# GpSimd makes both halves' low parts for some experts of the first expert pass

## The reference

```python
def ffn(x, Wg, bg, W1, b1, W2, b2):          # 4096 tokens of 128, 8 experts, hidden 256
    xf = x.reshape(-1, 128)
    probs = softmax(xf @ Wg + bg)
    w, idx = top_k(probs, 2); w = w / sum(w)
    comb = sum(one_hot(idx, 8) * w[..., None], axis=1)
    h = relu(einsum('nd,edh->enh', xf, W1) + b1[:, None, :])
    y = einsum('enh,ehd->end', h, W2) + b2[:, None, :]
    return einsum('end,ne->nd', y, comb)

x = x + long_convolution(layernorm(x))       # FFT over 256 positions, 16 sequences
x = x + ffn(layernorm(x))                    # first expert pass
x = x + attention(layernorm(x))              # 16 heads of 8, 4 query sets, causal
x = x + ffn(layernorm(x))                    # second expert pass
```

## Time and profile before

| | us |
|---|---|
| median of 3 runs | 857.32 (856.18 to 859.0) |
| the profiled execution, its own time | 855.01 |
| its span | 853.3 |
| TensorE busy | 801.8 (94%) |
| VectorE busy | 682.4 (80%) |
| ScalarE busy | 719.8 (84%) |
| GpSimd busy | 550.3 (64%) |

### The profile page before, as it was taken

The page is one execution under the profiler, slowest core; times in us unless marked ns, Lnnn a source line. Parts: engine busy times, 40 slices in busy tenths (PEclk is TensorE's granted clock), DMA queues, the critical chain, the costliest instruction groups (busy, mean ns, idle before and its releaser), DMA issues.

```text
span 853.3 us, 20661 instructions
## 1 busy us (share of the span) xinstructions
PE 801.8 (94%) x7793; PEld 446.1 (52%) x7793; DVE 682.4 (80%) x2000; ACT 719.8 (84%) x919; POOL 550.3 (64%) x620
## 2 busy tenths in 40 slices
PE   5899898989999999999999999999999999999995
PEld 4644475666677623333333333333333677777774
DVE  6898699999998766777777777778736899888884
ACT  7640488778888899999999999999998889999984
POOL 1187455535553498988899888888887555454542
PEclk9999999999999999999999999999999999999998
DMA  8201100000003334343334433433420000000000
GB/s 263 69 1 49 50 2 1 2 2 2 2 1 77 95 70 98 87 86 89 100 101 100 100 96 90 97 87 91 98 41 2 1 14 15 14 14 14 14 14 17
DMA packets 38521, 46.20 MB, mean 54 GB/s; under 512 B 6696, under 2 KB 24368, under 8 KB 38416
## 3 DMA queue, kind: packets, MB, share of 16 engines
q1 hardware_dynamic: 38416, 44.83, 20.8%
HBM read 28.03 MB, written 16.78 MB: 53 GB/s over the span
## 4 chain that ended last, share of the span: by engine, by line
PE 61%; ACT 14%; DVE 13%; issue 9%; POOL 3%; SPq 0%; DMA 0%; ACTq 0%
PE psum L816 16%; PE psum L762 15%; PE psum L1114 12%; ACT prob L1072 11%; PE psum L1063 5%; PE psum L1172 4%; DVE mixed L828 3%; DVE normed L351 2%; PE psum L566 2%; POOL prob L1087 2%; ACT decay L420 1%; PE psum L956 1%; PE psum L533 1%; PE psum L637 1%; DVE hidden_parts_first L785 1%
## 5 line engine op out<-in xcount | busy, mean ns | idle before, releaser
L1072 ACT ACTIVATE prob<-psum 128x1536 f32<-128x1536 f32 x256 | 347.7, 1500 | 15.5 <-PE psum L1063 15.5
L1114 PE MATMUL psum<-prob,vstack 128*32 128x256 f32 (+1 forms) x2048 | 204.9, 495 | 1.6 <-DVE o_tok L1122 1.6
L762 PE MATMUL psum<-xt_parts,w_parts 128*128 128x512 f16 x768 | 186.6, 379 | 0.0
L828 DVE SCALAR_TENSOR_TENSOR mixed<-psum,comb_y,mixed 128x128 f32<-128x128 f32 x512 | 143.1, 339 | 2.1 <-PE psum L816 2.1
L792 POOL TENSOR_TENSOR hidden_parts_second<-hidden_second,hidden_parts_second 128x512 f16<-128x512 f32 x64 | 78.9, 1233 | 91.8 <-ACT hidden_parts_second L778 91.8
L792 POOL TENSOR_TENSOR hidden_parts_first<-hidden_first,hidden_parts_first 128x512 f16<-128x512 f32 x64 | 77.9, 1222 | 77.7 <-ACT hidden_parts_first L778 77.5
L776 ACT ACTIVATE hidden_first<-psum,b 128x512 f32<-128x512 f32 x128 | 88.3, 690 | 29.1 <-PE psum L762 22.0
L1082 POOL TENSOR_SCALAR_AFFINE_SELECT prob<-prob 128x512 f32<-128x512 f32 x128 | 82.4, 644 | 41.0 <-ACT prob L1072 35.5
L1063 PE MATMUL psum<-qstack,kstack 32*128 32x512 f16 x768 | 99.7, 385 | 9.7 <-POOL prob L1087 4.8
L1063 PEld LDWEIGHTS psum<-qstack,kstack 32*128 32x128 f16 x768 | 24.9, 91 | 158.2 <-ACT prob L1072 139.8
L816 PE MATMUL psum<-w_parts,hidden_parts_first 128*128 128x128 f16 x1536 | 96.0, 219 | 10.5 <-DVE mixed L828 5.7
(11 more groups left out here) (121 smaller groups left out, 1101.1 us busy)
## 6 DMA issues: line engine op xcount, KB each, us to landing
qstack<-qk_parts SPq DMA_DIRECT2D x128, 128.0 KB, 3.6
qk_parts<-parts SPq DMA_DIRECT2D x64, 192.0 KB, 3.2
kstack<-qk_parts SPq DMA_DIRECT2D x128, 32.0 KB, 3.5
stream<-L_attn_a_u SPq DMA_DIRECT2D x4, 512.0 KB, 8.4
kept_x<-stream SPq DMA_DIRECT2D x4, 512.0 KB, 2.6
out<-mixed SPq DMA_DIRECT2D x8, 256.0 KB, 2.3
w_whole<-L_ffn_W SPq DMA_DIRECT2D x1, 1024.0 KB, 7.6
taps<-c_taps SPq DMA_DIRECT2D x1, 640.0 KB, 9.8
```

The source lines that it names most:

```text
L762: last = e.matmul(bank(u % 4), m.w1[:, w_part, ex, cols], xt_parts[:, s, x_part, :], start=(n == 0), stop=(n == len(PRODUCTS) - 1))
L828: last = e.scalar_tensor_tensor(out=m.y[:, t0 + t, :], in0=bank(down_bank(m, i))[:, t * P:(t + 1) * P], scalar=comb_y[:, s, t, ex:ex + 1], ...
L1072: e.activation(prob[:, n % PROBS, :], psum[:, TILE * (n % 2):TILE * (n % 2 + 1)], ACT.Exp, scale=SCALE)\
L1114: last = e.matmul(to[SLOT * lane:SLOT * (lane + 1)], vstack[:, b % 2, keys, first:first + SLOT], weights_of(n - t, lane, keys, pair), star ...
```

## The change

For some experts of the first pass GpSimd makes the low parts of both halves with one instruction of 128x1024 elements, which counts `low_both_halves`, and VectorE's instruction is left out. These are experts 3 and 6 in chunks 0 to 5, and experts 1, 3, 5 and 7 in chunks 6 and 7, 20 of 64. GpSimd's instruction keeps its place in the queue and its wait for the second half's relu. TensorE waits for the one semaphore instead of the two; where it waits for the two, it counts only the experts that use them. The second pass is as before.

```diff
--- before.py
+++ after.py
@@ -287,6 +287,7 @@
     combt_up, combt_copied, base_up, based = (sem(n) for n in ("comb_t_up", "comb_t_copied", "base_up", "based"))
     hid_up, relued, low_first, low_second, down_up, accum = (sem(n) for n in (
         "hidden_up", "relued", "low_first_half", "low_second_half", "down_up", "accumulated"))
+    low_both = sem("low_both_halves")
     STEPS = 14
     STACK = 2 * 2 * LANES * 16
 
@@ -778,8 +779,20 @@
                 last = e.activation(m.hidden_parts[:, r, 0, k, :], bank(u % 4), ACT.Relu, scale=scale, bias=bias)
             last.then_inc(relued, 1)
 
+
+    def both_on_gpsimd(i):
+        ch, ex = divmod(i, EXPERTS)
+        return ch < FFN_CHUNKS and (ex in (3, 6) if ch < FFN_CHUNKS - 2 else ex % 2 == 1)
+
+    def lows_before(i):
+
+        alone = sum(both_on_gpsimd(n) for n in range(i + 1))
+        return i + 1 - alone, alone
+
     def vector_low(e, m, ch, ex):
         i = (m.at + ch) * EXPERTS + ex
+        if both_on_gpsimd(i):
+            return
         r = i % HRING
         e.wait_ge(relued, HBLK * i + 1)
         e.tensor_tensor(m.hidden_parts[:, r, 1, 0, :], m.hidden[:, r, 0, :], m.hidden_parts[:, r, 0, 0, :],
@@ -789,8 +802,12 @@
         i = (m.at + ch) * EXPERTS + ex
         r = i % HRING
         e.wait_ge(relued, HBLK * i + 2)
-        e.tensor_tensor(m.hidden_parts[:, r, 1, 1, :], m.hidden[:, r, 1, :], m.hidden_parts[:, r, 0, 1, :],
-                        ALU.subtract).then_inc(low_second, 1)
+        if both_on_gpsimd(i):
+            e.tensor_tensor(m.hidden_parts[:, r, 1], m.hidden[:, r], m.hidden_parts[:, r, 0], ALU.subtract)\
+             .then_inc(low_both, 1)
+        else:
+            e.tensor_tensor(m.hidden_parts[:, r, 1, 1, :], m.hidden[:, r, 1, :], m.hidden_parts[:, r, 0, 1, :],
+                            ALU.subtract).then_inc(low_second, 1)
 
     def down_bank(m, i):
 
@@ -803,8 +820,12 @@
             e.wait_ge(relued, HBLK * (i + 1))
             terms = [(m.hidden[:, r, k], m.w2[:, ex * HBLK + k, :]) for k in range(HBLK)]
         else:
-            e.wait_ge(low_first, i + 1)
-            e.wait_ge(low_second, i + 1)
+            shared, alone = lows_before(i)
+            if both_on_gpsimd(i):
+                e.wait_ge(low_both, alone)
+            else:
+                e.wait_ge(low_first, shared)
+                e.wait_ge(low_second, shared)
             terms = [(m.hidden_parts[:, r, h_part, k], m.w2[:, w_part, ex * HBLK + k, :])
                      for k in range(HBLK) for h_part, w_part in PRODUCTS]
         if i >= 2:
```

## The result

The kernel after takes 864.5 us (median of 6 runs, 862.8 to 867.7), the kernel before 857.0 beside it (6 runs): ratio 1.0089, 95% interval 1.0067 to 1.0112. It is 7.5 us slower; the forecast was 867.6, 10.3 slower.

The account below looks back on a forecast made before the run. TensorE was taken to set the pace, with VectorE nearly full and partly waiting for GpSimd. Terms 5.1 + 3.2 + 0 + 1.0 + 1.0 = 10.3 us on a median of 857.3 gave 867.6 us, range 857 to 872.

Parts of the forecast that it names:

- What bounds the pass, and the lock: First expert pass: TensorE sets the pace, VectorE is nearly full and partly stands still until GpSimd's instruction ends.
- The exception kept from the earlier trace: GpSimd's rstd (L345) ran 1.05 us while two-input VectorE work (L683) passed; kept as ground for a rival.
- The joined instruction: GpSimd's 1024-element subtraction takes 2.13 us, 0.97 more than the 1.16 of a single half.
- the cheaper rival: Joined instruction at 1.7 us, so places cost about 0.5 each: 3.5 us slower, 861; chance 0.16.
- Expert 3, the first place: Chunks 1 to 5: L666 held 0.97 longer, routing chain 1.2 us late, L712 on TensorE 0.5 late.
- Expert 6, chunks 3 to 5: GpSimd's joined part delays VectorE's four L351 and what follows: 1.7 us a chunk, 5.1 for three.
- The new hole at down(7): Chunk 3: TensorE's down product of expert 7 waits for late L828 of expert 5, starting at 201.25, not 199.56.
- Chunks 1 and 2: Delays 1.24, 0.97 and 0.95 less 1.56 won from the blocked L785: 1.6 us late each, 3.2 together.
- Chunk 0, 6 and the end: Chunk 0 costs 0, at most 0.2; chunk 6 costs 1.0; the last down product in chunk 7 is 1.0 late.
- "faster": Rival: GpSimd lets VectorE in between the joined instruction's halves; 3.2 us won, 854.1; chance 0.13.
- "A wash": Rival: VectorE's saved 13.6 us and the added locks cancel everywhere but the last place: 858.3; chance 0.09.
- the hole at down(5): Chunks 3 to 5: TensorE waits 1.07 us for GpSimd's low part, queued behind L343 waiting for VectorE's statistics.

Follow-up runs that it names:

- extralow2: Kernel before plus a second full-size GpSimd subtraction (128x512) ahead of expert 3's low part in chunks 0 to 5, VectorE keeping its half: 857.63 us (1.0022).
- split: Kernel after with each joined GpSimd instruction written as two of 512 elements, one behind the other: 861.39 us (1.0052 to the kernel before).
- extrapow: Kernel before plus a GpSimd power on 128x4 elements behind expert 3's low part in chunks 0 to 5: 858.58 us (1.0012).
- lasttwo: Kernel after with only chunks 6 and 7 joined (experts 1, 3, 5 and 7), other chunks as before: 860.83 us (1.0038 to the kernel before).
- no7: Kernel after with the last expert of chunk 7 as in the kernel before: 864.28 us (1.0097 to the kernel before).

## Why the prediction was right, and where not

- *What bounds the pass, and the lock*: right. L667 ended 0.03 us behind GpSimd's joined instruction, at 1.64 us as said. By the rule of the Trainium skill that was weighed (page SBUF — State Buffer, section "SBUF: two separate sides"), the hold lasts for the whole instruction; extralow2 and split agree, with ends within 0.04 us. The exception kept from the earlier trace rows holds too: in extrapow a power with two SBUF inputs held none of five two-input instructions, so for it the measurement decides against the rule.
- *The joined instruction*: 2.13 forecast, 2.145 measured. The slope of the earlier trace rows was the right source; the cheaper rival, at 1.70, is out. The estimate from the Trainium skill's page GPSIMD Engine Reference, section "Elementwise — side-by-side cycle accounting", 2.29, was too high.
- *Expert 3, the first place*: the mechanism was right to each instruction, but L698 was 1.0 late, not 1.2. The forecast let the chain go on at 188.1, with 0.96 left, and wrote 189.3 for the sum, which is 189.06; the 1.24 that it took on to chunks 1 and 2 follows from neither. Measured from the mark, the chain ended at 12.14 us, 11.13 before. L712 then is 0.35 late, not 0.5. At down(5) this place has cost 0.71, where the forecast had 0.9.
- *Expert 6, chunks 3 to 5*: 1.7 forecast, 1.34, 1.18 and 1.35 measured. The mis-sized term is the length of the four L351: they begin 0.62 late (forecast 0.57), but take 3.78, not 4.15. GpSimd's row ended 0.32 sooner than forecast: 0.17 from the chain, the rest since one low part starts before the row of the one ahead ends (196.93, 198.04: 1.11 apart at 1.15 long). Over three chunks 3.9 in place of 5.1. The new hole at down(7) came; that at down(5) did not grow beyond the lateness that reaches it.
- *Chunks 1 and 2*: 1.6 forecast, 1.30 and 1.14 measured. At L828 of expert 4 it is 1.29 in chunk 2: 1.01 for the first place (forecast 1.24), and 0.28 for all of 0.97 + 0.95 - 1.56 (forecast 0.36).
- *Chunk 0, 6 and the end*: 0, and 1.86 for the last two against 2.0; TensorE waits 0.93 longer at L713 of chunk 6 and 1.07 at the last down, and all of it stays. Right, and lasttwo and no7 show them apart.
- *Sum*: 8.2 in the pass against 10.3, and every term that isn't zero a little too large. The profiled executions differ by 9.15 us, the medians by 7.5. The clock blurs the medians (last section): at a mean granted clock of 0.997 executions of the kernel before took 854.8 to 855.6 us and those of the kernel after 862.8 and 863.3, some 8 us more, as the marks say. Of the 3.1 us by which the forecast lies above the median, 2.1 is the sum and 1.0 this scatter.
- *The rivals*: "faster" needed L666 to end within 0.7 us; it took 1.64. Made to let go in the middle (split), the change loses 4.6 us still (3.6 by the marks), so that rival's price was wrong too. It had the first place at nothing, chunks 3 to 5 at -0.35 and the end at 1.0. In split the second half catches one more instruction of the chain (L673, 0.79 us) and the next low part an earlier one than before (L691, 1.03), so that the chain ends 0.50 late; L352 takes 3.66 in chunk 3, not 3.01, so down(7) waits for VectorE; and chunks 6 and 7 cost 1.8. "A wash" is out.

What the prediction did not see: the hole at down(5) that it described, with the row of three low parts behind it, was worth 9.2 us, more than the change costs, and one number removes both.

## What to carry to other kernels

Where two engines share a lock, work moved from one to the other is paid by both: price it by what the receiver's instruction will catch, not by the giver's busy time, part of which is waiting for that lock. If it must be moved, keep the seams, so that the other engine's short instructions get in. And look first for an instruction that stands too early in a queue, waits there, and keeps ready work behind it from starting: here moving two small steps by one expert gave 9.2 us, while the moved work cost 7.5.

## What the runs showed of the hardware that was not expected

A GpSimd subtraction on tiles of 128x512 stops VectorE's casts (L667, 128x8), its instructions with two inputs in SBUF (L673, 128x4) and the one-input scalings (L352, 128x128) until it ends. It does not stop the accumulation L849, one of whose two tiles is in PSUM: the four from 202.84 took 1.11 us beside a low part from 202.88 to 204.03. A GpSimd power of 128x4, over 1 us long, stops no two-input instruction (extrapow).

TensorE's granted clock dips right behind the pass in seven of the fourteen profiled executions, and this blurs the medians. In extrapow's profiled execution (window; PE, PEld, VectorE, ScalarE, GpSimd busy; granted clock; DMA share; GB/s):

```profile
296.34:301.34 5.00, 2.71 (x19) 1.03 (x18) 2.92 (x14) 4.56 (x4) 3.86 (x7) 0.79 0.47 128
301.34:306.34 5.00, 5.00 (x35) 1.10 (x33) 1.38 (x2) 3.77 (x3) 4.36 (x7) 0.53 0.33 71
306.34:311.34 5.00, 5.00 (x53) 1.60 (x50) 3.56 (x7) 4.62 (x4) 3.63 (x5) 1.00 0.02 3
```

0.53 is near the 1.2 GHz level (0.5 of 2.4). It fell where attention starts, with TensorE busy 2.71 of 5 us after a full pass. In the kernel after, the first 5 us of that stage are as idle (2.52), and the clock stayed at 1.00. What is behind the last mark took 559.06 us in extrapow, 559.05 in no7 (0.81 there), and 557.29 and 557.47 in the kernels before and after, with no dip. The other runs fit: of the 35 runs of the kernel before beside extrapow, those with a mean granted clock of 0.997 took 854.8 to 855.6 us, those with 0.989 took 859.2 to 859.6. This is the likely reason why extrapow's median lies 1.3 us above before's (its interval reaches below 1) with all intervals of the pass equal. What decides whether it dips was not found.
